# Table writes issued from ScalarE's queue, one stage for each image, in place of the sync engine's

## The chip, the cores and the metric

One core of a Trainium2 chip runs the whole program in one launch. The metric is the device time in microseconds (us). The engines are named as the profile names them: PE is TensorE (its weight loads are PEld), DVE is VectorE, ACT is ScalarE, POOL is GpSimd, SP is the sync engine, which computes nothing and issues DMAs. A name with a q (SPq) is an engine's instruction queue.

## The reference

Three parts follow one another for each of 32 images of 64 channels and 128 x 128 pixels, and a text of 128 tokens.

```
q_feat  = bilinear_sample(x, 32 x 32 grid)                 # 1024 queries an image
queries = q_feat @ W_q.T
h       = gelu(layer_norm(q_feat @ W_o1 + b_o1)); off = h @ W_o2 + b_o2
sampled = bilinear_sample(x, grid + 4 * off)               # 8 points a query
keys, values = sampled @ W_k.T, sampled @ W_v.T            # softmax over the 8 points
h = concat(attention over the points, txt)                 # 1024 + 128 tokens of 64
h = h + causal_attention(layernorm(h))
h = h + layernorm_affine(y + top-2 of 16 experts(y)),  y = layernorm(h)
```

## The kernel before

The images go in 16 pairs. The pipeline is written out by hand: in each repeat of it ("period") five pieces of work on up to four pairs are interleaved. For the pair after the current one the grid part runs; for the current one the sampled points ("tokens") and the attention of image 0; for the one before it the attention of image 1, the routing and the first expert groups; for the one before that the remaining expert groups, the fetches and the last norm. The strings in TURNS give the order of one period on each engine, one letter a stage: g is the grid part, x the experts, t, k, w, v and p the tokens, a, s and q the attention, c the scatter, f the fetch, e the end. LAST holds the order of the last periods, in which no grid part is left.

The change lies in the grid part. An image pair comes in 8 chunks of 16 rows. For each chunk SP loads two half chunks into `fm` (load_rows), PE turns them four rows at a time (rows_turn), ACT copies them from PSUM into `rows` (copy_rows), and the pixels are written to a table in HBM, as rows of 128 numbers that hold a pixel and the one below it (write_table). From the same `rows` PE samples the grid (sample), and ACT copies the results on: `qf` (feature), `qft` (feature_t), then the query and the offsets' input (copy_query). The `rows` buffer is double, so a chunk's first copy waits for the table write two chunks back. POOL gathers the sampled points from the table with indirect DMAs once all 8 chunks are written, one period later.

SP issues every direct DMA: the fm loads, the table writes (two of 1 MB a chunk, one for each image), the expert loads (`wx` is the weights of four experts in four DMAs, each behind a read of the expert's number; `xg` is the tokens), the stores of the experts' results (`ys_d`), text and output. POOL issues the indirect ones: 128 gathers, 32 scatters (`xs_d`) and 32 fetches (`ya`) a period. Each engine takes its instructions in the order written; a wait holds all that is behind it.

Lines: 658 load_rows, 676 the table write, 699 and 708 expert weights, 705 expert tokens, 707 the read of an expert's number, 715 the ys_d store; 816 rows_turn on PE, 827 sample, 1024 and 1032 the experts' two layers, 1048 ACT's copies.

Of the kernel before, what the change touches and what calls it, by code (L numbers as in the profile page):

```python
# [30 lines left out]
B, C, H, W = 32, 64, 128, 128  # L31
# [4 lines left out]
QT_N = NQ // P  # L36
# [7 lines left out]
CR = H // NCH  # L44
# [176 lines left out]
def grid_stages():  # L221

    order = [("load", (0,)), ("load", (1,))]
    for ch in range(NCH):
        for half in range(2):
            for g in range(2):
                order += [("rows", (ch, half, g)), ("copy_rows", (ch, half, g))]
            if ch < NCH - 1:
                order += [("load", (2 * ch + 2 + half,))]
        order += [("table", (ch,)), ("sample", (ch,)), ("feature", (ch,)),  # L230
                  ("turn_feature", (ch,)), ("feature_t", (ch,)), ("query", (ch,)), ("copy_query", (ch,))]
    return order + [*[("off_hidden", ())] * 23, ("off_exp", ()), *[("off_gelu", ())] * 3, ("off_turn", ()),
                    ("off_copy", ()), ("off_layer2", ()), *[("off_points", ())] * 8]


def first_gathers():

    return [("gather", (n,)) for n in range(NG)]
# [7 lines left out]
        "gsagxtqagqastgskgqsgasakgqaaqtqagqaagkgtgkaaggakgagtgkgtgkgtkgrgtgkgtgkgtgkgxgaagxtgxgkgaagxaatskxsk"  # L246
        "qxtsxaqsqagsagxqsksxxtxqsqatsqxasakqsxqasqaxaxsaqxtssqkxaakqtqaktxqaxatxkxkxtakaaxaxxx",
    "scalar":
        "xxttkxaagtkgtxagakaatgxagxvgaktagxvstxgqskgsxqggksxgqtgqxgsxgvtggsxgxkqtgkgqgtxxkqgxvqgtxkgstgqgsgqv"
        "tgqkgskqgqvqqgtgkgaagkagagaavtgkggtkggtkagtvkggtgkgteggktvgagagxagxagekgtavgaeagkxaasktgqsxqstqgksxq"  # L250
        "svxtqqsqxkseqtvqxeqeskxqqsktvqktqkvtxqxtkxkxatavaaakavxxa",
    "vector":
        "wawaaaaaaaaaaxaaaawwvwvwvxvvvvxvwwvvvvaaxavvaaavavavxavavawaavwavvxwawaxvvavvwvxvwavvvvvxavaawvaavaa"
        "vwaavvavavvaavvvwvaavaaaaaaaaaaaaaavweevevevveevvaaeaawaaeaaevaveeavveaavvaeeeerweeeveaavveavwaaeaae"
# [3 lines left out]
    "gpsimd":  # L258
        "pppppppffffffffffffffffpfffffffffpfffffpfcfccccccccpcccccccccccccccccccccccppppp",
    "sync":  # L260
        "ggxgxxxggxxxggxgxxghxxxgxggxxgggxghxggggggggexxxxxexxxxx",
}
LAST = {
    "tensor":
# [26 lines left out]
def strands():  # L291

    def part(stages, *names):
        return [s for s in stages if s[1] in names]

    tokens = [("tokens", *s) for s in token_stages()]
    attention = [(thread, *s) for thread, b in (("second", 1), ("first", 0)) for s in attention_stages(b)]
    split = {"s": part(attention, "score", "soft"), "q": part(attention, "turn_probs", "copy_probs")}
    pieces = {"t": part(tokens, "turn", "turned"), "k": part(tokens, "key_values", "copy_kv"),
              "w": part(tokens, "weigh", "weigh_rest"),  # L300
              "v": part(tokens, "scores", "point_exp", "values", "stats"),
              "p": part(tokens, "gather") + [("gather", *s) for s in first_gathers()]}
    return {**pieces, **split,
            "a": [s for s in attention if s not in split["s"] and s not in split["q"]],
            "h": [("text", "text", (b,)) for b in range(2)],
            "g": [("grid", *s) for s in grid_stages()],
            "r": [("route", *s) for s in route_stages()],
            "c": [("experts", *s) for s in scatter_stages()],
            "x": [("rest", *s) for s in expert_stages(range(FIRST_PART, MG))]
            + [("experts", *s) for s in expert_stages(range(FIRST_PART))],  # L310
            "f": [("fetch", *s) for b in range(2) for s in fetch_stages(b)],
            "e": [("end", *s) for b in range(2) for s in end_stages(b)]}
# [50 lines left out]

def build(nc, x, txt, w, out, tables):
    _, LOW, _ = grid_coordinates()
    ctx = ExitStack()
    with ctx:
        def sb(name, shape, dt=F32):
            return ctx.enter_context(nc.sbuf_tensor(name, shape, dt))
# [3 lines left out]
        def sig(name, per, spare=0):  # L373
            s = Signal(ctx.enter_context(nc.semaphore(name)), per, spare)
            signals.append(s)
            return s
# [20 lines left out]
        rows = sb("rows", [P, 2, 2, CR + 1, C])  # L397
        qf = sb("qf", [P, P])
        qft = sb("qft", [P, P])
        query = sb("query", [P, 2, QT_N, 2, C])  # L400
# [78 lines left out]
        def bank(n, a=0, b=BANK):  # L479
            return ps[:, n * BANK + a:n * BANK + b]  # L480
# [7 lines left out]
        rows_sb = sig("rows_sb", 4 * NCH)  # L488
        carry = sig("carry", NCH)
        table_in = [sig(f"table_in{n}", 32 * NCH // 2, 16) for n in range(2)]  # L490
# [12 lines left out]
        wcorn = [sig(f"wcorn{n}", 2 * QT_N, 24) for n in range(2)]  # L503
# [68 lines left out]
        def follow(engine, stages, k, pair, par):  # L572

            who = threads_of(pair, par)
            for thread[0], stage, args in period_order(k, engine, stages):
                stages[stage](*who[thread[0]], *args)
            thread[0] = None

        def follow_last(engine, stages):

            for k, name, stage, args in last_order(engine, stages):
                thread[0] = k, name
                stages[stage](*threads_of(Pair(k), k % 2)[name], *args)
            thread[0] = None

        def drive(eng, engine, stages, stretch):

            stretch(0, None)
            thread[0] = "grid"
            for stage, args in grid_stages() + first_gathers():  # L590
                if stage in stages:
                    stages[stage](Pair(0), 0, *args)
            for k in range(PAIRS - 1):
                stretch(1 + k, None)
                follow(engine, stages, k, Pair(k), k % 2)
            stretch(PAIRS, None)
            follow_last(engine, stages)
            stretch(PAIRS + 1, None)
# [15 lines left out]
        tab_v = [t.rearrange("(b y x) c -> b y x c", y=H, x=W) for t in tables]  # L614
# [5 lines left out]
        def _(sp):  # L620
# [36 lines left out]
                    sp.wait_ge(*rows_ps.rise(pair - 1, 4 * NCH - 2 * (1 - hc)))  # L657
                sp.dma_start(fm[:, hc % 2, :], x_v[pair.times(1), :, hc, :]).then_inc(fm_in[hc % 2].sem, 16)

            def write_table(pair, par, ch):  # L660

                sp.wait_ge(*rows_sb.rise(pair, 4 * (ch + 1)))
                sp.wait_ge(*carry.rise(pair, ch + 1))
                if ch == 0:

                    for n in range(2):
                        sp.wait_ge(*wcorn[n].rise(pair - 2, 2 * QT_N))
                n = CR if ch else CR - 1
                first = 0 if ch else 1
                y0 = ch * CR + first - 1  # L670
                for b in range(2):
                    src = rows[:, ch % 2, b, first:first + n, :]
                    src = bass.AP(tensor=src.tensor, offset=src.offset,
                                  ap=[list(src.ap[0]), [C, n], [1, 2 * C]])
                    dst = tab_v[par][b, y0:y0 + n].rearrange("y x c -> x y c")
                    sp.dma_start(dst, src).then_inc(table_in[ch % 2].sem, 16)

            def text(pair, par, b):

                sp.wait_ge(*ln_x.rise(pair - 1, 6 * b + 6))  # L680
                sp.dma_start(h0[:, b, QT_N, :], txt[pair.times(2, b)]).then_inc(txt_in[b].sem, 16)
# [35 lines left out]
            for t in tab_v:  # L717
                for b in range(2):
                    sp.dma_start(t[b, H - 1, :, :], zeros[:, 0:2 * C]).then_inc(spare_rows.sem, 16)
            drive(sp, "sync", {"load": load_rows, "table": write_table, "text": text, "store": store,  # L720
                       "expert_load": expert_load, "expert_store": expert_store}, unseen)
            sp.wait_ge(*stored.rise(Pair(PAIRS), 0))

# [322 lines left out]
        def _(act):  # L1046
            def copy(dst, src):
                return act.activation(dst, src, ACT.Copy)  # L1048

            def copy_rows(pair, par, ch, half, g):  # L1050
# [17 lines left out]
                if n == 3:  # L1068
                    act.sem_inc(carry.sem, 1)

            def feature(pair, par, t):
                act.wait_ge(*qf_ps.rise(pair, t + 1))
                copy(qf[:], bank(3, 0, P)).then_inc(qf_sb.sem, 1)
# [107 lines left out]
            def expert_relu(pair, par, g):  # L1181
# [3 lines left out]
            act.wait_ge(*tables_in.rise(Pair(0), 32))  # L1185
            copy(lower[:], prod[0][:, 0:P + 1]).then_inc(act_own, 1)
            act.wait_ge(*setup.rise(Pair(0), 1))
            drive(act, "scalar", {"copy_rows": copy_rows, "feature": feature, "feature_t": feature_t,
                        "copy_query": copy_query, "off_exp": off_exp, "off_copy": off_copy,
                        "turned": turned, "point_exp": point_exp, "copy_kv": copy_kv, "normalize": normalize,  # L1190
                        "copy_tokens": copy_tokens, "copy_q": copy_q, "copy_k": copy_k, "copy_v": copy_v, "soft": soft,
# [5 lines left out]
        def _(dve):  # L1197
# [270 lines left out]
            def scale(pair, par, b, k):  # L1468
                settle()
                _, ab = halves(k)  # L1470
                own(stt(ab[:, 2], ab[:, 2], 0.25, ab[:, 2], ALU.mult, ALU.mult))
                step(stt(ab[:, 1], ab[:, 1], 1.0 / C, ab[:, 2], ALU.mult, ALU.add))
                yield
                settle()
                step(ts(ab[:, 1], ab[:, 1], EPS, ALU.add))
                yield
                settle()
                yield from rsqrt(ab[:, 3], ab[:, 1], ab[:, 2])
                stt(ab[:, 4], ab[:, 0], -0.5, ab[:, 3], ALU.mult, ALU.mult).then_inc(
                    end_ab.sem if k == 2 else ln_ab.sem, 1)  # L1480
# [274 lines left out]
```

## Time and profile before

| | |
|---|---|
| median of 3 timed runs | 4535.47 us (4533.03 to 4543.56) |
| the profiled execution | 4544.44 us, span 4542.4 us |
| busy: PE, PEld | 3747.4 us (82%), 3260.8 us (72%) |
| busy: DVE, ACT, POOL | 3052.3 us (67%), 2231.7 us (49%), 3032.9 us (67%) |
| DMA packets of direct DMAs | 805768, 598.22 MB, 44.0% of the 16 DMA engines' span |
| DMA packets of indirect DMAs | 132432, 307.74 MB, 22.9% |
| table writes | 256, of 1024 KB (224) and 960 KB (32) |

Busy is the time in which an engine's own instructions run; issuing a DMA does not count as busy. A row of waits names the instruction that waited, what ended the wait, the total in us, how many times, and the longest. A row of the timeline has start and duration in us, the engine, the line, the operation, what it writes and reads, how many instructions in a row are put together (xN), and in brackets how long the engine was idle before it and what ended that.

### The profile page before, as it was taken

How to read it: one execution, taken by the hardware profiler on the slowest of the kernel's cores; microseconds unless marked ns; L12 is line 12 of the kernel's file. 1: busy time of each engine (PE TensorE's matmuls, PEld its weight loads, DVE VectorE, ACT ScalarE, POOL GpSimd, SP SyncE). 2: the span in 40 equal slices, each digit the busy share in tenths (PEclk: the TensorE clock that was granted, in tenths of full speed). 3: DMA queues.
4: the chain of work that ended last, by engine and by line, in shares of the span. 5: the costliest groups of instructions: out<-in, count | busy, mean ns of one | idle time of the engine just before them, and what ended most of it. 6: DMA issues, size and time to landing. Idle time of an engine off the chain costs nothing.

```text
span 4542.4 us, 82922 instructions
## 1 busy us (share of the span) xinstructions
PE 3747.4 (82%) x26592; PEld 3260.8 (72%) x26592; DVE 3052.3 (67%) x9244; ACT 2231.7 (49%) x5378; POOL 3032.9 (67%) x3089
## 2 busy tenths in 40 slices
PE   4577888888889888898988888898888888888863
PEld 2466777777777777787877777787777877777752
DVE  0485758677685867768585776858576685877432
ACT  2355545454555545454554545455454545554411
POOL 0666567767776777767676776767677676777152
PEclk9888989898998988898898988999798989988855
DMA  8759586684958578594857858585776848562322
GB/s 249 226 185 264 165 245 204 199 270 140 286 150 272 178 225 252 155 285 142 266 168 235 245 174 266 145 268 173 240 232 180 261 139 266 174 187 74 97 83 60
DMA packets 938629, 911.26 MB, mean 201 GB/s; under 512 B 121306, under 2 KB 822362, under 8 KB 938072
## 3 DMA queue, kind: packets, MB, share of 16 engines
q1 hardware_dynamic: 805768, 598.22, 44.0%
q0 software_dynamic: 132432, 307.74, 22.9%
q8 instruction: 218, 3.57, 0.3%
q14 instruction: 211, 1.73, 0.1%
HBM read 583.69 MB, written 323.53 MB: 200 GB/s over the span
## 4 chain that ended last, share of the span: by engine, by line
POOL 30%; PE 26%; issue 13%; SPq 10%; DMA 10%; DVE 7%; ACT 4%; POOLq 0%; DVEq 0%; ACTq 0%
POOL gath L762 13%; POOL ya L794 10%; POOL xs_d L778 7%; PE ps L1024 4%; PE ps L1032 4%; PE ps L885 3%; DMA fm<-in_x 3%; SPq L707 3%; PE ps L871 3%; DMA wx<-w_d 3%; PE ps L816 2%; SPq L708 2%; PE ps L942 2%; DMA ys_d<-yx 2%; SPq L715 2%
## 5 line engine op out<-in xcount | busy, mean ns | idle before, releaser
L762 POOL DMA_INDIRECT gath<-table,idx x2048 | 1995.9, 975 | 936.4 <-issue 635.1
L794 POOL DMA_INDIRECT ya<-ys_d,row x512 | 498.3, 973 | 373.2 <-DMA ys_d<-yx 211.6
L1232 DVE TENSOR_TENSOR prod<-gath,ps 128x1024 f32<-128x1024 f32 x512 | 617.6, 1212 | 161.0 <-DMA gath<-table,idx 128.1
L871 PE MATMUL ps<-const,prod 128*128 128x128 f32 x4096 | 610.0, 298 | 96.7 <-DVE prod L1232 94.6
L778 POOL DMA_INDIRECT xs_d<-xm,row x512 | 529.1, 1033 | 182.1 <-issue 152.9
L885 PE MATMUL ps<-w_kv,samp_t 128*128 128x128 f32 x4096 | 607.5, 296 | 29.6 <-ACT kv_sb L1048 17.3
L871 PEld LDWEIGHTS ps<-const,prod 128*128 128x128 f32 x4096 | 531.2, 157 | 117.3 <-DVE prod L1232 99.4
L885 PEld LDWEIGHTS ps<-w_kv,samp_t 128*128 128x128 f32 x4096 | 552.4, 209 | 62.1 <-issue 39.6
L1024 PE MATMUL ps<-xgt,wx 65*128 65x128 f32 x2560 | 419.5, 315 | 145.8 <-DMA wx<-w_d 95.7
L1024 PEld LDWEIGHTS ps<-xgt,wx 65*128 65x128 f32 x2560 | 370.9, 222 | 194.9 <-issue 114.6
L942 PE MATMUL ps<-k_t,q_t 128*128 128x512 f32 (+3 forms) x960 | 435.2, 537 | 77.0 <-DVE att L1496 51.8
L816 PE MATMUL ps<-const,fm 128*128 128x128 f32 x2048 | 362.0, 306 | 159.7 <-ACT rows L1048 73.3
L1032 PEld LDWEIGHTS ps<-wx,hx 128*128 128x128 f32 x2560 | 392.3, 231 | 78.7 <-ACT hx L1183 50.4
L1048 ACT ACTIVATE rows<-ps 128x512 f32<-128x512 f32 x512 | 304.3, 594 | 265.8 <-PE ps L816 262.5
L1048 ACT ACTIVATE samp_t<-ps 128x512 f32<-128x512 f32 x512 | 304.2, 594 | 264.5 <-PE ps L871 256.8
L1032 PE MATMUL ps<-wx,hx 128*128 128x64 f32 x2560 | 403.8, 312 | 26.5 <-ACT hx L1183 26.4
L1496 DVE CUSTOM_DVE_ANT_0 probs<-ps,const 128x512 f32<-128x512 f32 (+3 forms) x480 | 264.8, 552 | 229.0 <-PE ps L942 227.9
L964 PEld LDWEIGHTS ps<-v_sb,probs_t 128*128 128x128 f32 x2880 | 374.1, 197 | 55.3 <-issue 39.6
L816 PEld LDWEIGHTS ps<-const,fm 128*128 128x128 f32 x2048 | 267.0, 160 | 202.2 <-issue 90.5
L1232 DVE TENSOR_TENSOR yx<-ps,wx 128x256 f32<-128x256 f32 x320 | 134.4, 420 | 385.5 <-PE ps L1032 385.1
L964 PE MATMUL ps<-v_sb,probs_t 128*128 128x64 f32 x2880 | 385.6, 274 | 8.8 <-DVE h L1240 5.9
L1183 ACT ACTIVATE hx<-ps 128x512 f32<-128x512 f32 x320 | 191.0, 597 | 403.8 <-PE ps L1024 400.3
(169 smaller groups left out, 6270.6 us busy)
## 6 DMA issues: line engine op xcount, KB each, us to landing
table<-rows SPq DMA_DIRECT2D x224, 1024.0 KB
fm<-in_x SPq DMA_DIRECT2D x256, 512.0 KB
wx<-w_d SPq DMA_DIRECT2D x768, 128.0 KB
gath<-table,idx POOLq DMA_INDIRECT x2048
wx<-w_d SPq DMA_DIRECT2D x64, 512.0 KB
table<-rows SPq DMA_DIRECT2D x32, 960.0 KB
xg<-xs_d SPq DMA_DIRECT2D x192, 130.0 KB
ys_d<-yx SPq DMA_DIRECT2D x192, 128.0 KB
```

Source lines behind the costliest of these rows:

```text
L762: pool.indirect_dma_start(out=gath[:, n % NG, p, :], out_offset=None, in_=tables[par], in_offset=bass.IndirectOffsetOnAxis(ap=idx[:, par, ...
L778: pool.indirect_dma_start(out=xs_d[par], out_offset=bass.IndirectOffsetOnAxis(ap=row[:, par, j:j + 1], axis=0), in_=xm[:, par, s // QT_N, ...
L794: pool.indirect_dma_start(out=ya[:, k, t, :], out_offset=None, in_=ys_d[par], in_offset=bass.IndirectOffsetOnAxis(ap=row[:, par, n:n + 1], ...
L816: last = pe.transpose(bank(3, r * P, r * P + P), fm[:, half, (4 * g + r) * W:(4 * g + r + 1) * W], ident)
L871: last = pe.matmul(bank(0, p * P, p * P + P), prod[h][:, (p * 2 + dx) * P:(p * 2 + dx + 1) * P], ident, is_transpose=True, start=(dx == 0) ...
L885: last = pe.matmul(bank(1, p * P, p * P + P), samp_t[n % 2][:, (4 * h + p) * P:(4 * h + p + 1) * P], w_kv[:], start=True, stop=True)
L942: pe.matmul(bank(4, 0, m), q_t[:, i * P:(i + 1) * P], k_t[:, a:a + m], start=True, stop=True).then_inc(s_ps.sem, 1)
L964: last = pe.matmul(bank(7, (i % 8) * C, (i % 8) * C + C), probs_t[n % 3][:, (k % 4) * P:(k % 4) * P + P], v_sb[:, k, :], start=(k == 0), s ...
L1024: last = pe.matmul(bank(2, n * P, n * P + P), weights_of(g)[0:XW, n, 0:F], xgt[0:XW, m * P:m * P + P], start=True, stop=True)
L1032: last = pe.matmul(bank(2, n * C, n * C + C), hx[:, n * P:n * P + P], weights_of(g)[:, n, F:F + C], start=True, stop=True)
L1048: return act.activation(dst, src, ACT.Copy)
L1232: return dve.tensor_tensor(o, a, b, op)
```

## The change

SP's stage write_table is gone, and ACT has it. It is split: the write of image 0 stands in front of feature, the write of image 1 between feature_t and copy_query. What it waits for is as before, on image 0's stage alone. The order strings follow: ACT's gets a g more for each stage, SP's loses the g of each write. The bytes, their layout and the semaphores that others wait on are the same.

```diff
-        order += [("table", (ch,)), ("sample", (ch,)), ("feature", (ch,)),
-                  ("turn_feature", (ch,)), ("feature_t", (ch,)), ("query", (ch,)), ("copy_query", (ch,))]
+        order += [("table", (ch, 0)), ("sample", (ch,)), ("feature", (ch,)), ("turn_feature", (ch,)),
+                  ("feature_t", (ch,)), ("table", (ch, 1)), ("query", (ch,)), ("copy_query", (ch,))]
...
     "sync":
-        "ggxgxxxggxxxggxgxxghxxxgxggxxgggxghxggggggggexxxxxexxxxx",
+        "ggxgxxxgxxxggxxxghxxxgxgxxggxghxggggexxxxxexxxxx",
...
-            def write_table(pair, par, ch):
-
-                sp.wait_ge(*rows_sb.rise(pair, 4 * (ch + 1)))
-                sp.wait_ge(*carry.rise(pair, ch + 1))
...
-                for b in range(2):
...
-                    sp.dma_start(dst, src).then_inc(table_in[ch % 2].sem, 16)
...
+            def write_table(pair, par, ch, b):
+
+                if b == 0:
+                    act.wait_ge(*rows_sb.rise(pair, 4 * (ch + 1)))
+                    act.wait_ge(*carry.rise(pair, ch + 1))
+                    if ch == 0:
+
+                        for n in range(2):
+                            act.wait_ge(*wcorn[n].rise(pair - 2, 2 * QT_N))
+                n = CR if ch else CR - 1
+                first = 0 if ch else 1
+                y0 = ch * CR + first - 1
+                src = rows[:, ch % 2, b, first:first + n, :]
+                src = bass.AP(tensor=src.tensor, offset=src.offset,
+                              ap=[list(src.ap[0]), [C, n], [1, 2 * C]])
+                dst = tab_v[par][b, y0:y0 + n].rearrange("y x c -> x y c")
+                act.dma_start(dst, src).then_inc(table_in[ch % 2].sem, 16)
```

On ACT, at one chunk of a period in which the experts run beside it, before (qf and query are the grid part, hx and xgt the experts', samp_t the tokens', probs and probs_t the attention's):

```order
L1183 ACTIVATE hx<-ps 128x512
L1048 ACTIVATE qf<-ps 128x128
L1048 ACTIVATE probs_t<-ps 128x384
L1048 ACTIVATE samp_t<-ps 128x512
L1048 ACTIVATE qft<-ps 128x128
L1048 ACTIVATE probs_t<-ps 128x512
L1048 ACTIVATE xgt<-ps 65x512
L1048 ACTIVATE query<-ps 128x128
```

The same place on ACT in the changed kernel:

```order
L1183 ACTIVATE hx<-ps 128x512
L1069 DMA table<-rows 128x16x128
L1030 ACTIVATE qf<-ps 128x128
L1030 ACTIVATE probs_t<-ps 128x384
L1030 ACTIVATE samp_t<-ps 128x512
L1030 ACTIVATE qft<-ps 128x128
L1030 ACTIVATE probs_t<-ps 128x512
L1030 ACTIVATE xgt<-ps 65x512
L1069 DMA table<-rows 128x16x128
L1030 ACTIVATE query<-ps 128x128
```

Two DMA issues came in, in front of qf and of query; nothing else of ACT moved (its lines are 18 less, for the function taken out above it).

On SP, between two expert groups of the same period, before:

```order
L708 DMA wx<-w_d 128x256
L676 DMA table<-rows 128x16x128 [waits carry,rows_sb]
L676 DMA table<-rows 128x16x128
L715 DMA ys_d<-yx 128x256 [waits yx_sb]
L705 DMA xg<-xs_d 128x260 [waits yx_sb]
L707 TENSOR_LOAD eid
```

The same place on SP in the changed kernel:

```order
L690 DMA wx<-w_d 128x256
L697 DMA ys_d<-yx 128x256 [waits yx_sb]
L687 DMA xg<-xs_d 128x260 [waits yx_sb]
L689 TENSOR_LOAD eid
L689 ISA x2
```

The two writes and their wait are gone; the store of one group and the loads of the next follow the loads before them.

## Rows read from the trace of the kernel before

**Rows 1.** The page, the chain that ended last, by engine.
```profile
POOL 30%; PE 26%; issue 13%; SPq 10%; DMA 10%; DVE 7%; ACT 4%; POOLq 0%; DVEq 0%; ACTq 0%
```

**Rows 2.** Windows, eight repeats; the header names the columns.
```profile
core 0: us, PE busy (x) PEld busy (x) DVE busy (x) ACT busy (x) POOL busy (x), PEclk, DMA share, GB/s
1281.00:3382.00 2101.00, 1822.08 (x13295) 1598.70 (x13294) 1511.94 (x4615) 1107.30 (x2688) 1514.68 (x1536) 0.89 0.72 215
```

**Rows 3.** Waits from 1281 to 3382 us, PE and ACT: total us, times, longest.
```profile
ACT hx L1183 <- PE ps L1024: 180.1, 116, 5.2
...
PE ps L1024 <- DMA wx<-w_d: 55.6, 33, 3.8
...
PE ps L903 <- ACT xm L1128: 29.9, 36, 1.4
...
PE ps L816 <- ACT rows L1048: 28.3, 16, 4.5
...
PE ps L816 <- DMA fm<-in_x: 16.8, 8, 2.8
...
PE ps L1024 <- ACT xgt L1048: 14.9, 20, 1.0
```

**Rows 4.** Waits of POOL in the same stretch.
```profile
POOL gath L762 <- DVE prod L1232: 80.5, 17, 13.4
...
POOL ya L794 <- DMA ys_d<-yx: 29.7, 8, 4.7
```

**Rows 5.** Timeline of SP, 1687.4 to 1687.8 us.
```profile
1687.49 0.38 SPq L676 DMA_DIRECT2D table<-rows  x1
```

**Rows 6.** Timeline of SP, one expert phase.
```profile
1677.30 0.33 SPq L715 DMA_DIRECT2D ys_d<-yx  x1
...
1687.49 3.38 SPq L676 DMA_DIRECT2D table<-rows  x2
1690.92 2.91 SPq L715 DMA_DIRECT2D ys_d<-yx  x1
1693.89 1.23 SPq L705 DMA_DIRECT2D xg<-xs_d  x1
1696.86 4.13 SPq L708 DMA_DIRECT2D wx<-w_d  x4
1701.03 0.43 SPq L658 DMA_DIRECT2D fm<-in_x  x1
```

**Rows 7.** Timeline of PE, the same phase: its waits for expert weights.
```profile
1657.22 1.13 PE L1024 MATMUL ps<-xgt,wx 65*128 65x128 f32 x8 [1.07 <-DMA wx<-w_d]
...
1690.30 1.13 PE L1024 MATMUL ps<-xgt,wx 65*128 65x128 f32 x8 [2.25 <-DMA wx<-w_d]
...
1703.52 2.05 PE L1024 MATMUL ps<-xgt,wx 65*128 65x128 f32 x8 [3.36 <-DMA wx<-w_d]
```

**Rows 8.** The chain from 1687 to 1704 us, by line.
```profile
by line: SPq L676 19.6%; DMA wx<-w_d 18.8%; SPq L715 17.1%; SPq L707 14.4%; issue 10.1%; SPq L708 9.9%; SPq L705 7.2%; PE ps L1024 3.2%; SPq L663 0.1%
```

**Rows 9.** Line 676, all table writes: SP's time for one in ns, min/median/max.
```profile
L676 SPq DMA_DIRECT2D table<-rows x256: 359/1670/15455, 23.3 to 3897.7; - x128
```

**Rows 10.** Timeline of SP, three later pairs of table writes.
```profile
1726.79 6.47 SPq L676 DMA_DIRECT2D table<-rows  x2
...
1763.96 5.24 SPq L676 DMA_DIRECT2D table<-rows  x2
...
1779.15 4.12 SPq L676 DMA_DIRECT2D table<-rows  x2
```

**Rows 11.** Timeline of ACT, qf and query of the same three chunks.
```profile
1726.72 0.28 ACT L1048 ACTIVATE qf<-ps 128x128 f32<-128x128 f32 x1 [0.36 <-PE ps L827]
...
1731.82 0.28 ACT L1048 ACTIVATE query<-ps 128x128 f32<-128x128 f32 x1
...
1765.38 0.28 ACT L1048 ACTIVATE qf<-ps 128x128 f32<-128x128 f32 x1
...
1768.10 0.26 ACT L1048 ACTIVATE query<-ps 128x128 f32<-128x128 f32 x1
...
1780.83 0.26 ACT L1048 ACTIVATE qf<-ps 128x128 f32<-128x128 f32 x1
...
1783.02 0.27 ACT L1048 ACTIVATE query<-ps 128x128 f32<-128x128 f32 x1
```

More of the change, by code:

```diff
@@ L248 @@
     "scalar":
-        "xxttkxaagtkgtxagakaatgxagxvgaktagxvstxgqskgsxqggksxgqtgqxgsxgvtggsxgxkqtgkgqgtxxkqgxvqgtxkgstgqgsgqv"
-        "tgqkgskqgqvqqgtgkgaagkagagaavtgkggtkggtkagtvkggtgkgteggktvgagagxagxagekgtavgaeagkxaasktgqsxqstqgksxq"
-        "svxtqqsqxkseqtvqxeqeskxqqsktvqktqkvtxqxtkxkxatavaaakavxxa",
+        "xxttkxaagtkgtxagakaatgxaggxvgaktaggxvstxgqskgsxqggksxggqtgqxggsxgvtggsxgxkqtggkgqggtxxkqgxvqgtxkgstg"
+        "qggsgqvtggqkgskqgqvqqgtgkggaagkaggagaavtgkggtkgggtkaggtvkggtgkgtegggktvggagagxagxagekggtavgaeaggkxaa"
+        "sktgqsxqstqgksxqsvxtqqsqxkseqtvqxeqeskxqqsktvqktqkvtxqxtkxkxatavaaakavxxa",
     "vector":
@@ L658, in load_rows @@
                 sp.dma_start(fm[:, hc % 2, :], x_v[pair.times(1), :, hc, :]).then_inc(fm_in[hc % 2].sem, 16)
-            def write_table(pair, par, ch):
-                sp.wait_ge(*rows_sb.rise(pair, 4 * (ch + 1)))
-                sp.wait_ge(*carry.rise(pair, ch + 1))
[L664 to L670, printed above, removed]
-                for b in range(2):
[L672 to L675, printed above, removed]
-                    sp.dma_start(dst, src).then_inc(table_in[ch % 2].sem, 16)
             def text(pair, par, b):
@@ L719, in _ @@
                     sp.dma_start(t[b, H - 1, :, :], zeros[:, 0:2 * C]).then_inc(spare_rows.sem, 16)
-            drive(sp, "sync", {"load": load_rows, "table": write_table, "text": text, "store": store,
+            drive(sp, "sync", {"load": load_rows, "text": text, "store": store,
                        "expert_load": expert_load, "expert_store": expert_store}, unseen)
@@ L1187, in _ @@
             act.wait_ge(*setup.rise(Pair(0), 1))
-            drive(act, "scalar", {"copy_rows": copy_rows, "feature": feature, "feature_t": feature_t,
+            drive(act, "scalar", {"copy_rows": copy_rows, "table": write_table, "feature": feature, "feature_t": feature_t,
                         "copy_query": copy_query, "off_exp": off_exp, "off_copy": off_copy,
```

## The prediction

> **What bounds the kernel now.** I read the page's chain first, then one long repeating stretch by windows, then the waits of PE, POOL and ACT in it, then single instructions of SP and ACT. Of the chain that ended last POOL holds 30%, PE 26% and SP's queue 10% [rows 1]. SP computes nothing, so a tenth of the chain on it is unusual. The stretch from 1281 to 3382 us holds eight repeats of the pipeline, 262.6 us each (2101 / 8): PE works 227.8 us of each, ACT 138.4 [rows 2]. No engine is full, and the order on each is fixed, so a late operand costs what it makes PE or POOL stand.
>
> Over these eight repeats PE stands 55.6 us for expert weights (wx) and 16.8 for image rows (fm): 72.4 us, or 9.1 a repeat, for loads that SP issues. For three products of ACT it stands 29.9 + 28.3 + 14.9 = 73.1 us, also 9.1 a repeat; ACT stands 180.1 us for one product of PE alone [rows 3]. POOL waits 29.7 us for SP's ys_d stores and 80.5 us for DVE's release of a gather buffer: 13.8 a repeat [rows 4].
>
> The table writes are one reason for SP's lateness. The first of a pair is off SP's hands in 0.38 us [rows 5]; the pair takes 3.38 us from 1687.49, and then a ys_d store takes 2.91 and an xg load 1.23 where an undisturbed ys_d takes 0.33 and a load 0.43 [rows 6]. So a DMA behind a write is held until the one ahead of it has been taken in. The four weight loads behind them are out by 1700.99 (1696.86 + 4.13), and PE has nothing to do until 1703.52 [rows 7]. In the chain from 1687 to 1704 us SP's table line holds 19.6% and its ys_d line 17.1% [rows 8].
>
> **The change part by part.**
>
> *SP loses 256 issues.* A pair and what it holds up behind it costs SP about 3.38 + (2.91 - 0.33) + (1.23 - 0.43) = 6.8 us at the place shown. The waits before it go as well. What PE can get back is bounded by rows 3: nothing, if the loads are late for another reason, and 9.1 us a repeat, if all were late for this one. Each group's four loads still follow one another on SP: 4.13 us from the first to the end of the last [rows 6]. Only half of the eight pairs of a repeat stand among expert loads; the others stand in front of fm loads. In one expert phase PE stood for wx 1.07, 2.25 and 3.36 us [rows 7]: the last lay behind a table pair on SP, the second fell in the time in which a pair moved its 2 MB, the first had no write near it. That is half for certain and 84% with the second; I take 70% of 9.1, so 6.4 us a repeat. POOL's ys_d wait, 3.7 us a repeat, falls in the same time and is not added.
>
> *ACT gains 256 issues.* The trace has no DMA issued by ACT. The nearest rows are SP's own of the same transfer: 0.36 at the least, 1.67 in the median, 15.46 at the most [rows 9]. A write that finds none ahead should cost about 0.38 us. That is 16 x 0.38 = 6.1 us of ACT a repeat. The first of a pair stands in front of the qf copy and has its cover only where ACT waits there for PE.
>
> *The second write is a stage of its own.* It stands in front of the query copy. If ACT's queue behaves as SP's, it is held until the first has been taken in, so what counts is the pair's length on SP against ACT's time from qf to query. In the repeat I followed these are 6.47 against 5.10, 5.24 against 2.72, and 4.12 against 2.19 us [rows 10, 11]; take off 0.4 for the second's own issue, and 1.0 + 2.1 + 1.5 = 4.6 us are left. In the other five pairs of that repeat ACT's distance is the longer in the same views. So ACT loses 6.1 + 4.6 = 10.7 us of 262.6, where it has 124.2 us idle. What reaches PE lies between nothing (ACT waits for PE more than PE for it, [rows 3]) and all of it. PE already stands 9.1 us a repeat for ACT, so the cover is thin in places: I take a quarter, 2.7 us. If ACT's issue took the median of 1.67 us instead of 0.38, the loss would be 26.7 us a repeat before the same quarter: 6.7, and all of the gain would be gone.
>
> *Waits that move.* The write's waits for rows and carry are for ACT's own earlier copies; behind the waiting write stand qf, samp_t, probs_t and kv copies, for which PE waits. PE's sampling waits for the same last rows copy, so qf could not start at once either. The wait for the old table's readers at chunk 0 is for work two pairs back and costs nothing; if it did not, all of ACT would stand.
>
> *Traffic.* The bytes are the same. The DMA engines are busy 0.72 of the repeats [rows 2]. Loads no longer stand behind a write of 1 MB in one queue, but share the engines with it and with POOL's gathers; a gather can land later than now. I put no term on it: at worst POOL's and DVE's waits take back some of the gain, which the range holds.
>
> *Sum.* 6.4 - 2.7 = 3.7 us a repeat. There are 15 repeats with table writes: -55.5 us. The start, eight chunks of the first pair with nothing else running, gets 8 second writes on a serial path of rows, sample and query, at the 0.6 us of above (4.6 / 8), all of it on the path: +5. The last 600 us have no table write: 0. The profiled execution took 4544.4 us (span 4542.4), so 4494; the median of the timed runs is 9 below it, which gives 4485 us.
>
> The Trainium skill has a sentence against this change. By *DMA: Bandwidth & Descriptors*, section "Issuing engines are not separate DMA queues", issuing from several engines saves only the sequencer's time for the issue, usually small beside the transfer. The trace agrees with the first half only: the time saved is SP's, but with 3 to 6 us a pair it is not small. By the rule's second half the gain would be the plain issue time, 16 x 0.38 us of an SP that is not full, and the result would be a loss of ACT's 2.7 us a repeat.
>
> **Rivals.**
>
> *A. The generator of descriptors is shared, nothing is won.* What holds the second write may not be SP's queue, but what feeds the DMA engines for both queues. Then an SP load that follows an ACT write by less than its length is still held, and ACT's write is held by SP's loads. For it: the hold also falls on small stores behind a write [rows 6]. Against it: with the pair apart each hold is one write, about half. Price: half of 6.4 is left, 3.2; ACT pays 2.7 and about 0.5 more for holds of SP's making: nothing a repeat and +5 at the start, so about 4540. The skill's section "Queues, rings and completion order" of the same page says that SP and ACT each have rings of their own, but no descriptor generator of their own; no row here can show that, since only SP issues on that path.
>
> *B. ACT's stalls reach PE whole: slower.* In the attention part ACT feeds PE at every step, and a stall of 0.4 to 2.5 us at qf or query moves the probs and hx copies behind it. It decides once over 6.4 / 10.7 = 60% of ACT's loss reaches PE. With all of it: (10.7 - 6.4) x 15 + 5 = +70, about 4605. For it: PE's 9.1 us a repeat for ACT. Against it: ACT idles 47% of the repeat.
>
> *C. More comes back than PE's own waits.* The expert groups form a path from scatter through SP, PE and DVE to POOL's fetches that returns every repeat. If it and not PE's order sets the repeat, POOL's 13.8 us go: -207, about 4328. Against it: 80.5 of the 110 us there are waits for DVE, which the change leaves.
>
> **How the numbers follow.** Forecast 0.55, own range 4430 to 4520; A 0.17; B 0.18; C 0.10. The range of 4390 to 4585 leaves out the far half of B and most of C. Within 0.2% of 4535 (9 us either way, what a measurement here can tell from no change) I put 0.12: mostly A. Slower 0.24: B and a part of A. Faster 0.64: the forecast and C.
>
> **What the changed profile would show.** Right: SP's ys_d and xg issues back at 0.33 and 0.43 us; PE's waits for wx and fm in eight repeats down from 72.4 to under 25 us; the repeat near 259 us; ACT's first writes near 0.4 us and the second ones 0.4 to 2.5; PE's waits for ACT up by 10 to 30 us in eight repeats. Wrong: SP's small issues still at 1 to 3 us right after a write of ACT (A); PE's waits for xm, rows, xgt and probs_t up by over 60 us in eight repeats (B); gathers that land so late that DVE's prod waits for them much more than now (traffic). A first write on ACT that takes well over 0.4 us would break the second term at its root.

## The result and the profile after

The changed kernel is slower: a median of 4564.67 us (4548.54 to 4586.5, 12 runs) against 4530.37 (4508.27 to 4543.56, 12 runs) for the kernel before beside it, a ratio of 1.0088 with a 95% interval of 1.0069 to 1.0107. The forecast was 4485 us and faster. The profiled execution took 4574.5 us, span 4572.6: 30.2 us over the span of before.

The page shows first where the writes went: queue 10 is ScalarE's, and it now moves the table (columns: packets, MB, share of the 16 DMA engines' span).

```profile
q1 hardware_dynamic: 281480, 331.86, 23.7%
q0 software_dynamic: 132432, 307.74, 22.4%
q10 hardware_dynamic: 524288, 266.35, 19.9%
```

The chain that ended last, by engine, answers [rows 1]:

```profile
POOL 31%; PE 28%; issue 14%; DMA 8%; SPq 7%; DVE 7%; ACT 4%; another core or an unknown queue 0%; ACTq 0%; POOLq 0%; DVEq 0%
```

SP's queue fell from 10% to 7%: the relief of SP took place. The same eight repeats end later. The first output store of a pair went out at 1281 and 3382 us before, and at 1282 and 3416 us after, so a repeat grew from 262.6 to 266.7 us (2134 / 8). Windows over those eight, for [rows 2], with the same columns:

```profile
1282.00:3416.00 2134.00, 1825.30 (x13297) 1600.90 (x13297) 1512.74 (x4618) 1108.23 (x2689) 1524.24 (x1538) 0.88 0.70 212
```

PE is busy 1825.30 us against 1822.08: the work is the same, so the 33 us are standing time. The waits of PE in these eight repeats say which, beside [rows 3]:

```profile
PE ps L1006 <- DMA wx<-w_d: 89.8, 32, 6.9
...
PE ps L798 <- DMA fm<-in_x: 15.9, 8, 3.6
PE ps L1006 <- ACT xgt L1030: 14.8, 20, 1.0
PE ps L798 <- ACT rows L1030: 12.2, 14, 1.6
PE ps L798 <- ACT o L1030: 12.1, 19, 1.2
...
PE ps L988 <- DMA xg<-xs_d: 9.6, 11, 2.7
```

The waits for expert weights rose from 55.6 to 89.8 us: no more often (33 and 32 times), but longer, with 6.9 us in place of 3.8 at the most. All PE waits for DMAs rose by 37.9 us (77.4 to 115.3, the sum of the rows of the view), those for ACT fell by 6.9 (114.7 to 107.8), those for DVE are the same (83.4, 83.9). That is +31.5, with +3.2 of busy time 34.7, against the 33 found. Over the whole run PE's waits rose by 42.8 us (724.0 to 766.8) and its busy time fell by 11.6, together 31.2, against 30.2 of span. In that rise are gains as well: the waits for wx rose by 58.5 us (95.7 to 154.2), those for fm fell by 33.9 and those for rows by 31.6. Up to the first of the eight repeats the two kernels are level (1281 and 1282 us), and behind the last the changed one is 4 us the shorter: the loss is made in the repeats.

POOL, for [rows 4]:

```profile
POOL gath L744 <- DVE prod L1232: 110.7, 21, 18.0
...
POOL ya L776 <- DMA ys_d<-yx: 3.5, 1, 3.5
```

The wait for ys_d stores is gone (29.7 to 3.5), and the one for DVE grew by as much (80.5 to 110.7): POOL waits about as long as before, for another engine, and the repeat got no shorter, so its wait for the stores did not set the repeat.

ACT's side is the source line of the table write (ns, min/median/max), beside [rows 9]:

```profile
L1069 ACTq DMA_DIRECT2D table<-rows x256: 366/366/6723, 18.1 to 3935.7; - x128
```

At least half of the writes took 0.366 us, the least seen, where on SP the median was 1.67. All 256 sum to 146 us of ACT, and 35 of them took over 0.6 us: all but one were second writes, among them all eight of the first pair (0.9 to 1.9 us).

How a group of loads suffers is seen in one place. This is the chain of waits from 1678 to 1692 us (start, length, what); L687 is the issue of xg, L689 the read of an expert's number from SBUF into SP's register, L690 the issue of a weight load.

```profile
1678.60 0.71 SPq L687
...
1679.36 0.27 SPq L689
...
1680.05 0.35 SPq L690
...
1680.45 0.27 SPq L689
...
1681.56 1.02 SPq L689
...
1683.41 1.22 SPq L689
...
1685.08 5.15 DMA wx<-w_d
...
1690.36 1.83 PE ps L1006 x7
```

And these are two of ACT's instructions in the same time, from its timeline, with what PE then did, from its own:

```profile
1679.63 0.37 ACTq L1069 DMA_DIRECT2D table<-rows  x1
1683.90 0.37 ACTq L1069 DMA_DIRECT2D table<-rows  x1
...
1690.36 2.04 PE L1006 MATMUL ps<-xgt,wx 65*128 65x128 f32 x8 [5.67 <-DMA wx<-w_d]
```

The write of image 0 went out in 0.37 us at 1679.63, between the first register read of a group and its first weight load. The first two reads took 0.27 us each; the third and the fourth, with the table's packets under way, 1.02 and 1.22. The fourth load, issued at 1685.08, 1.2 us after the second write, needed 5.15 us to release PE, which stood 5.67. Nothing waited for SP's queue to take a DMA in; the register reads and the transfer itself became slow. In the last 5 us of PE's wait, 1685 to 1690, the DMA engines were full (355 GB/s), and this is how they were shared (packets, MB, share of the 16 engines; q1 is SP's queue):

```profile
q10 hardware_dynamic: 1790, 0.91, 62.1%
q1 hardware_dynamic: 446, 0.41, 23.5%
```

The table's queue had 62.1% of them, SP's with the weights 23.5%.

Counted over the whole trace: I took each of the 192 groups from the start of its xg issue to 2 us after the end of its fourth weight issue, and call it met if over 50 KB of table packets started in that time. Before, 43 groups were met, and 6.4% of the table's packets fell in such a time; after, 74 and 26.0%. From the start of the xg issue to the end of the fourth weight issue a group not met took 5.0 us (median) in both kernels; one met took 5.2 before and 6.8 after. PE's wait for wx divides the same way, each wait put down to the group whose load ended it: the groups not met cost PE 47.5 us before (149 of them) and 44.0 after (118), the groups met 48.2 (43) and 110.1 (74). So all of the rise lies in the groups that a write met.

### The profile page after: what moved, and what is told of

The parts are those of the page before. It is cut to its first block, busy times and chain, and to the rows that moved or that the text cites. A ratio compares the mean times of both kernels' runs of the same rounds, so it can differ in the third digit from the quotient of the medians.

```text
span 4572.6 us, 82922 instructions
## 1 busy us (share of the span) xinstructions
PE 3735.8 (82%) x26592; PEld 3248.1 (71%) x26592; DVE 3051.9 (67%) x9244; ACT 2232.6 (49%) x5378; POOL 3045.8 (67%) x3089
## 3 DMA queue, kind: packets, MB, share of 16 engines
q0 software_dynamic: 132432, 307.74, 22.4%
## 4 chain that ended last, share of the span: by engine, by line
POOL 31%; PE 28%; issue 14%; DMA 8%; SPq 7%; DVE 7%; ACT 4%; another core or an unknown queue 0%; ACTq 0%; POOLq 0%; DVEq 0%
POOL gath L744 14%; POOL ya L776 9%; POOL xs_d L760 8%; PE ps L1006 4%; DMA wx<-w_d 4%; PE ps L1014 4%; SPq L689 3%; PE ps L867 3%; PE ps L853 3%; PE ps L798 3%; PE ps L924 3%; SPq L690 2%; DMA fm<-in_x 2%; PE ps L946 1%; ACT xm L1128 1%
## 5 line engine op out<-in xcount | busy, mean ns | idle before, releaser
L1006 PE MATMUL ps<-xgt,wx 65*128 65x128 f32 x2560 | 430.2, 321 | 201.3 <-DMA wx<-w_d 154.2
L1006 PEld LDWEIGHTS ps<-xgt,wx 65*128 65x128 f32 x2560 | 380.8, 227 | 250.3 <-issue 168.2
L1014 PEld LDWEIGHTS ps<-wx,hx 128*128 128x128 f32 x2560 | 392.5, 231 | 78.8 <-ACT hx L1183 51.2
```

The lines of the kernel that those rows point to most:

```text
L1006: last = pe.matmul(bank(2, n * P, n * P + P), weights_of(g)[0:XW, n, 0:F], xgt[0:XW, m * P:m * P + P], start=True, stop=True)
L1014: last = pe.matmul(bank(2, n * C, n * C + C), hx[:, n * P:n * P + P], weights_of(g)[:, n, F:F + C], start=True, stop=True)
```

## The experiments

The theory, after the traces (**overlap**): on SP a write stood in the same queue as the loads and, by SP's order, between groups; from ACT it goes out as soon as the rows are there, and its bytes run beside a group's reads, issues and loads. The rivals: **ACT's own time** (issues and holds in ACT's stream), and **pieces** (2048 pieces of 512 B a write, rather than its bytes, slow the other queue).

**Bytes or issues.** Four kernels in one series, with the kernel before at 4521.9 us (4505.21 to 4537.22). Two of them leave out most of the table's bytes (one row of pixels for each write from the third pair on, so the later samples are of old pixels), two move all bytes in two pieces of 4 KB a partition in place of 16 pieces of 512 B, which puts the pixels in other places of the table.

```diff
 e3_act_small, e4_sp_small (the second on the kernel before)
-                n = CR if ch else CR - 1
+                n = 1 if pair.off >= 2 else CR if ch else CR - 1
 e5_act_fat, e6_sp_fat (the second on the kernel before)
-                src = rows[:, ch % 2, b, first:first + n, :]
-                src = bass.AP(tensor=src.tensor, offset=src.offset,
-                              ap=[list(src.ap[0]), [C, n], [1, 2 * C]])
-                dst = tab_v[par][b, y0:y0 + n].rearrange("y x c -> x y c")
+                src = rows[:, ch % 2, :, first:first + n, :].rearrange("p b r c -> p b (r c)")
+                dst = tab_v[par][b, y0:y0 + n].rearrange("y x c -> (y x c)").rearrange("(p b k) -> p b k", p=P, b=2)
```

> The changed kernel, but from the third pair on each table write moves one row of pixels instead of 15 or 16 (64 KB instead of 1 MB); the rest of the table keeps older pixels. To be read against the same cut with SP as issuer. Theory 1 (the writes' traffic beside the expert loads): with the bytes gone the loss is gone, time 0 to 0.5% below that of SP's version. Theory 2 (ACT's own cost): still 0.6 to 1% above it.

> The kernel before with the same cut of its table writes to one row of pixels from the third pair on. Both theories: faster than before, since SP is no longer held by a write; by 0.5 to 3%, and its PE waits for wx and fm go down.

> The changed kernel with the same bytes a write, but each of 128 partitions gives two runs of 4 KB to one run of 8 KB of the table instead of 16 runs of 512 bytes; pixels land in other places of the table. It parts two forms of theory 1. If the number of pieces costs (512-byte pieces keep whatever makes them, or the DMA engines, busy beside the loads): the loss is gone, PE's waits for wx back to 40 to 60 us in eight repeats, time well under before. If it is the bytes alone: PE's waits for wx stay at 80 us or more and the ratio over 1.004.

> The kernel before with the same two 4 KB runs a partition in its table writes. It gives the reference for ACT's version. If pieces cost, SP's second write is held less than 3.7 us (1.5 us or less) and the time falls; ACT's version is then within 0.3% of this one. If bytes cost, the hold stays at 3 us or more.

| | median us | ratio to before (95%) | PE for wx, whole run |
|---|---|---|---|
| before, after (first series) | 4530.37, 4564.67 | 1.0088 (1.0069 to 1.0107) | 95.7, 154.2 |
| e3, ACT, few bytes | 4428.22 | 0.9783 (0.9755 to 0.9812) | 69.2 |
| e4, SP, few bytes | 4433.46 | 0.9808 (0.9782 to 0.9834) | 68.6 |
| e5, ACT, large pieces | 4574.1 | 1.0116 (1.0082 to 1.015) | 164.7 |
| e6, SP, large pieces | 4457.66 | 0.9856 (0.983 to 0.9882) | 78.5 |

With few bytes it makes no difference who issues: the intervals of e3 and e4 overlap, though ACT has all 256 issues (0.326 us each in the median) in e3. ACT's issue time alone is therefore not the cause: what it costs, if anything, is no more than what the same issues cost on SP. PE's waits for ACT say the same: 294.1 us in e3 and 290.3 in e4, 264.3 in e5 and 271.4 in e6. With all bytes in large pieces ACT's queue is 2.6% slower than SP's (1.0116 / 0.9856), more than with small pieces, where 0.3% at most was expected if pieces cost; so pieces are not the cause either. The waits of PE over the whole run, first of e5, then of e6:

```profile
PE ps L1006 <- DMA wx<-w_d: 164.7, 57, 8.7
```

```profile
PE ps L1022 <- DMA wx<-w_d: 78.5, 57, 3.3
```

The same number of waits, twice as long. And SP's hold, the reason for the change, is mostly due to the pieces: the write's line in e6 has a median of 0.608 us against 1.670 in [rows 9], and the second writes of the pairs one of 0.62 against 3.71.

```profile
L674 SPq DMA_DIRECT2D table<-rows x256: 512/608/7113, 23.4 to 3782.7; - x128
```

Of the 141.3 us between the profiled spans of e5 and e6 (4571.0, 4429.7) PE's waits are 78.5 (750.0 and 671.5) and its busy time is 62.6 (3750.5 and 3687.9, for the same matmuls). The mean granted clock was 0.867 in e5 and 0.881 in e6. So nearly half of it came as slower matmuls; why the clock was lower in the kernel that waits more, no run here takes apart. (The profiled run of e6 was the fastest of its six: between the medians lie 116.4 us.)

**Place in the repeat.** All other series fell where every kernel, that of before too, takes 1.6 times as long (7.2 ms; "another core or an unknown queue" holds 34 to 36% of the chain in e12 and e1d, which I cannot explain), so each ratio there is read within its series, and sizes do not carry over to the first. The kernel before was not traced there, so its wait for wx in these series is not known. e1d gives ACT the writes of chunks 4 to 7 and SP the others as before; e2d the other way round; e12 is the changed kernel again.

```diff
+        on_act = ch in ON_ACT       # (4, 5, 6, 7) in e1, (0, 1, 2, 3) in e2
+        order += [("act_table", (ch, 0)) if on_act else ("table", (ch,)), ("sample", (ch,)), ("feature", (ch,)),
+                  ("turn_feature", (ch,)), ("feature_t", (ch,))]
+        order += [("act_table", (ch, 1))] * on_act + [("query", (ch,)), ("copy_query", (ch,))]
```

> The changed kernel once more, beside the two halves of its change in the same series of runs. 1.007 to 1.013 of the kernel before. If the two halves are independent, what the next two kernels lose adds up to this within 0.4%.

> ScalarE writes chunks 4 to 7 alone. Overlap with the expert loads: 0.996 to 1.003, PE's wait for wx in 1281 to 3382 us near the 55.6 us of before. ScalarE's own time: half the loss of the changed kernel.

> ScalarE writes chunks 0 to 3 alone. Overlap: the whole loss of the changed kernel, PE's wait for wx 80 to 95 us in that stretch if the run is of the length of the first ones. ScalarE's own time: half the loss.

Measured: e12 1.0096 (1.0073 to 1.0119), e1d 1.0008 (0.9993 to 1.0024), e2d 1.0096 (1.0079 to 1.0113), with before at 7209.06 us. The half with chunks 0 to 3 loses as much as the whole change, the other half nothing clear of noise. PE's waits for wx in the whole run, of e12, e1d and e2d in turn:

```profile
PE ps L1006 <- DMA wx<-w_d: 75.3, 19, 6.2
```

```profile
PE ps L1027 <- DMA wx<-w_d: 19.6, 14, 2.2
```

```profile
PE ps L1027 <- DMA wx<-w_d: 78.8, 21, 6.3
```

Between e1d and e2d lie 59.2 us of this wait, and 56.9 us of median time (7276.76 less 7219.89). That the two are so near is no account of the time: between the two profiled spans lie 43.3 us (7218.1, 7261.4), of which PE's busy time is 33.3 (4185.7, 4219.0) and all its waits together 9.2, as others fell while that for wx rose. By the count described above, table packets of ACT's queue met 64 of the 192 groups in e12, 63 in e2d, and none in e1d. In e2d the 63 met groups hold 77.7 of the 78.8 us. SP's own writes met 52 groups in e1d, for 19.1 us in all, but with 396 KB in a met group on the average against 921 in e2d: how much of a write falls in a meeting seems to count, not only that they meet.

The two halves had been run in three earlier series of the same kind, e1 and e2, e1b and e2b, e1c and e2c.

> Chunks 4 to 7 of each pair are written from ACT in two stages, chunks 0 to 3 from SP as before. Theory 1 (overlap): the changed kernel loses because its writes run while an expert group's loads are issued and move; beside chunks 4 to 7 no expert row group runs, so nothing is lost and SP is relieved: ratio to before 0.997 to 1.001, PE's waits for wx in 1281 to 3382 us stay near 56 us. Theory 2 (ACT's own cost: 16 issues a repeat delay ACT's copies): half of the loss, ratio 1.003 to 1.006.

> Chunks 0 to 3 of each pair are written from ACT in two stages, chunks 4 to 7 from SP as before. Theory 1 (overlap with expert loads): the whole loss or more, ratio 1.008 to 1.014, PE's waits for wx near 90 us. Theory 2 (ACT's own cost): half of the loss, ratio 1.003 to 1.006.

> The same kernel as the first with ACT writing chunks 4 to 7 (the first comparison ran on a chip on which every kernel took 7.2 ms). Theory 1 (overlap with the expert loads): ratio 0.992 to 1.001, PE's waits for wx as before the change, those for fm lower. Theory 2 (ACT's own cost): 1.003 to 1.006.

> ACT writes chunks 0 to 3, SP 4 to 7. Theory 1: ratio 1.008 to 1.016, PE's waits for wx up by 50 us or more over the whole run. Theory 2: 1.003 to 1.006.

> ScalarE writes the table's chunks 4 to 7, the sync engine chunks 0 to 3. Theory of overlap (what costs time is a table write in ScalarE's queue that runs beside a group's expert rows and weights): no group of expert rows stands among the stages of chunks 4 to 7, so nearly none of the loss is here, 0.995 to 1.003 of the kernel before, PE's wait for wx in 1281 to 3382 us near its 55.6 us. Theory of ScalarE's own time (16 issues a repeat stand in its stream): half of the change's loss, about 1.004.

> ScalarE writes chunks 0 to 3, the sync engine chunks 4 to 7. Overlap: the whole loss of the changed kernel or more, 1.007 to 1.012, PE's wait for wx 80 to 95 us. ScalarE's own time: half of it, about 1.004, wx near 60.

Measured, in that order of series: 1.0003, 1.0017 and 1.0021 for chunks 4 to 7 (wx 17.7, 20.7, 19.0), 1.0079, 1.0093 and 1.0101 for chunks 0 to 3 (wx 79.3, 77.7, 82.6). For chunks 4 to 7 the second and third interval lie just above 1 (from 1.0004 and 1.0006), so a loss of 0.1 or 0.2% may be there; theory 1 had at most 1.001 in the second. Half of ACT's issues stand at either place: ACT's own time, if an issue costs the same wherever it stands, would have split the loss in two, and falls. My expectations' wx figures (near 55.6, and 80 to 95) were for the shorter runs; only the difference can be read.

**Register reads or landing.** e8 is the changed kernel, e9 the kernel before, both with expert numbers written into the program, so that the loads are the same in number and size, but of other experts than the router's.

```diff
-                    e = sp.value_load(eid[j + m:j + m + 1, par:par + 1], min_val=0, max_val=E - 1)
+                    e = (j + m) % E
```

> The changed kernel with the expert numbers written into the program (j + m modulo 16 in place of those that the router chose), so that the sync engine reads no register from SBUF ahead of a weight load; as many loads of the same size. If the table's packets cost by the register reads, this and the next kernel take the same time within 0.3%. If they cost by the landing of the weights (and their issue), this one stays 0.5 to 0.9% above the next.

> The kernel before with the same fixed expert numbers. Against the kernel before it shows what the register reads cost in all: the chain of a group is shorter by four reads of about 0.3 us each, so PE's wait for wx falls below 55.6 us, and the time by 0 to 0.8%.

Measured: e8 0.9916 (0.9897 to 0.9935), e9 0.9844 (0.9823 to 0.9865), in one series. PE's waits for wx, of e8 and then of e9:

```profile
PE ps L1006 <- DMA wx<-w_d: 28.9, 15, 3.6
```

```profile
PE ps L1024 <- DMA wx<-w_d: 1.4, 4, 0.6
```

Without any register read the changed kernel still loses 0.7% (0.9916 / 0.9844 = 1.0073, against 1.0096 with them), and the wait of 27.5 us that divides the two can only be late issue and late landing; it is half of the 54.4 us between their profiled spans. e9 gained 1.6% on the kernel before, where I expected 0.8% at most. A read costs SP more than its 0.3 us: from the start of the xg issue to the end of the fourth weight issue, a group not met took 5.1 us in e12 and 2.4 in e8, so 0.7 us a read with the register operations behind it. The reads add to the wait: with them it was 75.3 us in e12. How much of the loss is theirs, 0.2% by these ratios, is within the intervals.

**A later place for both writes.** e11 puts both of a chunk's writes behind copy_query on ACT, in all chunks.

```diff
-        order += [("table", (ch, 0)), ("sample", (ch,)), ("feature", (ch,)), ("turn_feature", (ch,)),
-                  ("feature_t", (ch,)), ("table", (ch, 1)), ("query", (ch,)), ("copy_query", (ch,))]
+        order += [("sample", (ch,)), ("feature", (ch,)), ("turn_feature", (ch,)), ("feature_t", (ch,)),
+                  ("query", (ch,)), ("copy_query", (ch,)), ("table", (ch, 0)), ("table", (ch, 1))]
```

> The changed kernel with both writes of a chunk in one place on ACT, right behind copy_query. Its second write finds the first one under way, so ACT should be held about 3.7 us in the median, 8 times a repeat, which the split avoids. Theory 1: the writes start some 4 us later, still among the expert loads, so that loss stays (ratio 1.005 or more), and ACT's hold comes on top. Theory 2 (ACT's own cost leads): far slower than the changed kernel, 1.03 or more, PE's waits for ACT up by over 100 us.

Measured: 1.0144 (1.0129 to 1.0158). Here ACT's queue does hold: the line of the write, and two waits of PE.

```profile
L1069 ACTq DMA_DIRECT2D table<-rows x256: 366/977/4008, 23.9 to 6406.8; - x128
```

```profile
PE ps L809 <- ACT rows L1030: 171.1, 37, 14.1
...
PE ps L1006 <- DMA wx<-w_d: 22.4, 14, 4.9
```

The second write right behind the first took 1.84 us in the median (128 of them, 269 us in all, where e12's second ones took 61), and PE's sampling stood 171.1 us for the last row copies against 79.4 in e12. The loss moved from the weights to ACT: 42 groups were still met, for 22.4 us of wx where e12 has 75.3, so of theory 1 the loss came true but not that it stays with the weights. It does not part overlap from hold, as both changed; it shows that the split of the write into two stages did its work in the changed kernel.

**Small writes beside SP's.** e7 keeps SP's writes and adds 256 DMAs of 1 KB on ACT, at the 16 places, to memory that nobody reads.

```diff
+            def act_table(pair, par, ch, b):
+                act.dma_start(spare[pair.off, ch, b], const[:, 0:2]).then_inc(spared.sem, 16)
```

> The kernel before with SP's table writes as they are, and on ACT at the 16 places a pair where the changed kernel issues its writes a DMA of 1 KB to a spare area that nobody reads. It has ACT's issues without their bytes. Theory 1 (overlap): ratio 0.999 to 1.002. Theory 2 (ACT's own cost): the issue is 0.37 us as with 1 MB, so the whole loss or most of it, ratio 1.006 to 1.010.

> SP's writes as they are and 256 DMAs of 1 KB more on ACT. Theory 1: 0.999 to 1.003. Theory 2 (an issue on ACT delays what follows on ACT): 1.006 to 1.015, with PE's waits for ACT up by 30 us or more.

Measured: 1.0149 (1.0125 to 1.0174), and 1.0151 (1.0129 to 1.0174) when repeated: more than the changed kernel loses in the same kind of run, for DMAs that took ACT 0.326 us each, 84 us in all (each goes out as 128 packets of 8 bytes). PE's wx waits were 37.0 and 33.1 us. This fits no theory well. It would take all of ACT's 84 us on the path, and more, where e1's 128 issues cost nothing and e3's 256 nothing against e4. e3 and e7 differ in that e7 has both sets of issues, and in the length of the runs. What e7 costs stays open, and with it whether ACT's own time has a part in the losses of this slower kind of run; in the first series PE's waits for ACT in the eight repeats fell.

## Why the prediction was wrong

**What bounds the kernel: right.** SP's lateness was real. With the writes gone SP's share of the chain fell, and its ys_d issues sum to 87 us against 164, its fm issues to 113 against 250. PE's waits for fm over the whole run fell from 60.4 to 26.5 us, most of it before 560 us, and for rows by 31.6. Not all the small issues were back at their least time: an xg issue of 1.50 us stands at 1686.29, 2.4 us after an ACT write, as rival A would have it.

**SP loses 256 issues: the step that failed.** "I take 70% of 9.1, so 6.4 us a repeat." 9.1 was the wait for wx and fm, and 55.6 of its 72.4 us was wx. That part did not fall but rose, by 34.2 us in eight repeats, 4.3 a repeat, and the repeat grew by 4.1. In place of a gain of 6.4 us there was a loss of 4.2 (the two waits together went from 72.4 to 105.7). The 70% came from one expert phase with three waits. Of these the last was read rightly: the pair's packets had moved by 1697, before the four loads behind it were out, so SP's queue had made them late. The second had the table's bytes under way, as the prediction said, and whichever queue issues them, the bytes are there. e4 shows how little was to be won over the whole run: with hardly any table bytes PE still waits 68.6 of the 95.7 us for wx, so the writes were behind some 27 us of it, or 28%, where the sum had them behind 70%.

**Traffic: priced at nothing, and it decided.** "The bytes are the same ... I put no term on it." The bytes were the same, their time was not. In SP's queue a write could not go out within a group of loads; in ACT's it can, and 74 groups met one in place of 43. I had looked for the price at the gathers, where it was small (DVE's waits for gathers: 48.1 us in the eight repeats before, 46.0 after), and not at the loads just freed.

**ACT gains 256 issues: right in the first part, too high in the second.** First writes took 0.37 us against 0.38. The second ones were seldom held in the repeats: the median is 0.37 as well, and all holds of the eight repeats sum to 8.3 us, 1.0 a repeat in place of 4.6. What reached PE there was less than the 2.7 us a repeat: all of PE's waits for ACT in eight repeats fell by 6.9 us. The start was priced about rightly: all eight second writes of the first pair were held, a chunk took 11.6 us in place of 11.1, and the second pair's first write came at 166.5 us against 159.0. What the prediction lacked is that this is won back, as PE waits less for fm: the fourth pair's first write came at 600 us against 607. Before 560 us PE's waits for qf rose from 9.9 to 23.8 us, with one of 14.7, and over the whole run its waits for ACT rose by 12.9 (302.5 to 315.4).

**The rivals.** B had the sign but not the mechanism: in the repeats, where the time was lost, PE's waits for ACT did not grow. A's mark, slow small issues right after a write of ACT, is seen in places, but A's price was a gain halved, not one turned round. C falls: POOL's wait for ys_d went and the repeat grew. The Trainium skill's page *DMA: Bandwidth & Descriptors*, section "Issuing engines are not separate DMA queues", which the prediction held against the change, came nearer: the engines share what carries the data, and what another issuer saves is issue time. The trace agrees in that the issue time saved, 582 us on SP for 146 on ACT, did not make the kernel faster; that the move could cost 0.9% is more than the rule says.

**What is shown and what is only argued.** Shown: the loss needs the table's bytes (e3 against e4), does not need them in small pieces (e5 against e6), comes from chunks 0 to 3 (four pairs of e1 and e2), goes with PE's wait for wx, and is there without the register reads (e8, e9). Read from the traces, with no kernel that changes it alone: that it is the meeting in time (all of the rise in PE's wait for wx lies in groups that a write met). Open: whether the same meeting within one queue would cost as much, or two queues divide the DMA engines otherwise than one. A kernel in which ACT's write keeps to SP's place between groups would part the two; it wasn't tried, since with the order of both engines fixed the two would wait for each other.

## What to carry to other kernels

A place in a busy queue can also keep a DMA's bytes apart from those of its neighbours: here 6.4% of the table's packets fell beside a group of loads from SP's queue, and 26.0% from ACT's. Before moving a bulk write to an idle queue, look at which small, urgent loads it will then run beside, and leave out its bytes in one experiment to see how much of their lateness is its doing (here 27 of 96 us). Where the queue is slow because a write has many small pieces, larger pieces in the same queue may be the better change: 1.4% here, with a table whose layout this kernel could not use as it stands.

## What the runs showed of the hardware

- SP's read of an expert's number from SBUF, 0.27 us, took 1.02 and 1.22 us while a write of ACT's queue moved its 1 MB. Summed over 768 reads it was 335 us after and 239 before, the longest 1.77 and 1.03.
- A 1 MB write in 2048 pieces occupied the issuing engine for 0.37 us where none was ahead of it in its queue; the one right behind it on ACT took 1.84 in the median (e11). In pieces of 4 KB an issue took 0.52 us on ACT at the least, more than the small pieces' 0.37.
- The queue did not have to be SP's: the hold of a write behind a write is seen on ACT as well. Its longest, 6.72 us at 380.15, is of a write issued 22.8 us behind the last one, whose bytes were still moving beside POOL's gathers. From 382 to 392 us the DMA engines took as many packets from POOL's queue (q0) as from ACT's (q10), so that the gathers, whose packets go up to 4 KB and over, moved 3.34 MB and the table, in packets of 512 B, 0.52 (packets, MB, share; in a short window the shares can add up to a little over 100%):

```profile
q0 software_dynamic: 1025, 3.34, 86.4%
q10 hardware_dynamic: 1025, 0.52, 17.5%
```
